# Inner activations as offset float16 integers turned by a DMA, and new instruction orders, in a one-core vision-transformer block

## What is computed

```python
h = patches(x) @ W.T + b                                   # 768 -> 256
c = h @ w1.T + b1
w = softmax((c @ ww.T + bw).reshape(..., 16, 31), -1)      # 16 heads, 31 taps along the image axis
a = layer_norm(h + (causal_tap_sum(w, c) @ w2.T + b2), gamma, beta)
h = _layernorm(h + a)
q1 = act_quant(h)                                          # per row: round(x * 127 / max|x|)
u = silu(q1 @ weight_quant(w_gate).T) * (q1 @ weight_quant(w_up).T)    # 256 -> 1024
out = _layernorm(h + act_quant(u) @ weight_quant(w_down).T)            # 1024 -> 256
```

## Time and profile before

| | us |
|---|---|
| median of 3 runs | 127.66 (127.19 to 128.3) |
| the profiled execution | 127.84 |
| its span, first to last instruction | 125.4 |
| busy in the span: TensorE, VectorE, GpSimd, ScalarE | 112.0, 92.7, 71.3, 65.2 |
| mean granted TensorE clock, share of full speed | 0.989 |

### The profile page before, as it was taken

One profiled execution on the slowest core, in us unless ns is written; L12 is line 12 of the kernel. 1 busy time (PEld: TensorE's weight loads), 2 busy tenths in 40 slices (PEclk: granted clock), 3 DMA queues, 4 the chain that ended last, 5 costly groups with the idle time before them and its releaser, 6 DMA issues.

```text
span 125.4 us, 2349 instructions
## 1 busy us (share of the span) xinstructions
PE 112.0 (89%) x722; PEld 72.2 (58%) x722; DVE 92.7 (74%) x240; ACT 65.2 (52%) x110; POOL 71.3 (57%) x123
## 2 busy tenths in 40 slices
PE   6999989999899999999999999999999984897600
PEld 2377456688358568555855677476676652663400
DVE  5029764387438929999998998996999989699740
ACT  0402139865030834856775469568554775686300
POOL 7990000209002488722886247498978488998870
PEclk9999999999999999999999999999999999999995
DMA  4999999932231011313330220222320001101112
GB/s 91 394 322 408 423 418 423 404 89 19 56 31 10 0 48 14 29 47 33 61 35 6 52 26 3 55 25 57 33 51 5 0 0 42 42 0 42 47 43 82
DMA packets 22313, 12.44 MB, mean 99 GB/s; under 512 B 18013, under 2 KB 20317, under 8 KB 21918
## 3 DMA queue, kind: packets, MB, share of 16 engines
q1 hardware_dynamic: 21504, 10.72, 29.8%
q10 hardware_dynamic: 798, 1.58, 3.9%
HBM read 9.95 MB, written 2.34 MB: 98 GB/s over the span
## 4 chain that ended last, share of the span: by engine, by line
POOL 23%; DVE 13%; PE 12%; issue 8%; ACT 2%; POOLq 1%; DVEq 0%; ACTq 0%
POOL gu L1031 6%; POOL rstd L969 6%; PE bank L400 3%; PE bank L383 3%; POOL f L1038 2%; POOL veps L968 2%; POOL res L1009 2%; PE bank L322 2%; DVE a L734 2%; POOL h L1018 2%; DVE sc L788 1%; POOL shift_out L1007 1%; DVE gu L782 1%; POOL h1b L1026 1%; DVE stats L740 1%
## 5 line engine op out<-in xcount | busy, mean ns | idle before, releaser
L322 PE MATMUL bank<-xT,tokW 128*128 128x256 f32 x96 | 22.8, 387 | 0.3 <-DMA tokW<-in_tokW 0.2
L322 PEld LDWEIGHTS bank<-xT,tokW 128*128 128x128 f32 x96 | 18.3, 194 | 4.7 <-DMA tokW<-in_tokW 1.6
L997 POOL TENSOR_TENSOR taps<-probs,inv_total 128x256 f32<-128x256 f32 x8 | 6.8, 854 | 21.0 <-DVE inv_total L709 21.0
L968 POOL TENSOR_SCALAR veps<-mv 128x1 f32<-128x1 f32 x24 | 5.0, 210 | 22.1 <-DVE mv L719 14.5
L400 PE MATMUL bank<-conv_w,vpad 128*32 128x128 f32 x256 | 15.7, 397 | 0.4 <-DMA conv_w<-shear 0.4
L969 POOL TENSOR_TENSOR rstd<-veps,minus_half 128x1 f32<-128x1 f32 x24 | 14.4, 599 | 2.0
L383 PE MATMUL bank<-wl,h1T 128*128 128x496 f32 x32 | 14.6, 579 | 0.0
L630 ACT ACTIVATE q2T<-bank,minus_magic 128x512 bf16<-128x512 f32 x15 | 10.3, 688 | 5.8 <-PE bank L493 5.7
L493 PE MATMUL bank<-ident,gu 128*128 128x128 f32 x64 | 9.6, 275 | 3.6 <-POOL gu L1031 2.2
L617 ACT ACTIVATE silu<-bank,sc 128x512 f32<-128x512 f32 x16 | 11.0, 687 | 2.7 <-PE bank L453 2.7
L400 PEld LDWEIGHTS bank<-conv_w,vpad 128*32 128x32 f32 x256 | 8.5, 122 | 6.6 <-DMA conv_w<-shear 1.7
(11 more groups left out here) (110 smaller groups left out, 231.1 us busy)
## 6 DMA issues: line engine op xcount, KB each, us to landing
xT<-in_xT SPq DMA_DIRECT2D x3, 768.0 KB, 16.1
w_raw<-in_wg SPq DMA_DIRECT2D x1, 1024.0 KB, 12.6
w_raw<-in_wu SPq DMA_DIRECT2D x1, 1024.0 KB, 14.6
w_raw<-in_wd SPq DMA_DIRECT2D x1, 1024.0 KB, 16.5
shear<-taps SPq DMA_DIRECT2D x8, 128.0 KB, 1.9
conv_w<-shear SPq DMA_DIRECT2D x64, 16.0 KB, 1.9
out_dram<-res SPq DMA_DIRECT2D x8, 128.0 KB
xT<-in_xT ACTq DMA_DIRECT2D x2, 384.0 KB, 5.5
```

The lines of the kernel that those rows point to most:

```text
L322: last = nc.tensor.matmul(ps_embed(pair, m), tokW[:, k, m * P:(m + 1) * P], xT[:, pair, k, :], start=(k == 0), stop=(k == KC_PATCH - 1))
```

## The change

Quantised values are now float16 integers plus 1536 (`STEP`), exact in that type, and all quantised weights and turned activations are float16. For tiles 0 to 5 GpSimd writes q2 (float16) and SP turns the whole 128x1024 tile by one transposing DMA from SBUF to SBUF, straight into q2T; the offset stays in it, and `down` opens with a product of one row, -1536 times the column sums of the down weights, which `down_sums` makes once. Tiles 6 and 7 still go over TensorE, in float16. `centre` moves to ScalarE with its sign turned, the gate and down weights are rounded, clipped and finished on GpSimd, the scale arithmetic is written shorter with a small instruction more on GpSimd (`inner_limit` and the end of `inv_std_mid`), silu is written into `gu`, the first embedding runs by chunks of the inner dimension, and all lists are written anew. The diff, cut to its core:

```diff
-LATE = 5
-WARM_UP = 10
+TP = 6
+WARM_UP = 6
+STEP = 1536.0
 @block.sync
-            sp.dma_start(tokW[:, 0:3, :], tokW_d[:, 0:3, :]).then_inc(tokW_in[0], 16)
-            sp.dma_start(tokW[:, 3:6, :], tokW_d[:, 3:6, :]).then_inc(tokW_in[1], 16)
-            sp.dma_start(w1o[:], w1o_d).then_inc(w1o_in, 16)
+            for k in range(KC_PATCH):
+                sp.dma_start(tokW[:, k, :], tokW_d[:, k, :]).then_inc(tokW_in[k], 16)
+            def turn(t):
+                sp.wait_ge(q2_ok, 2 * t + 2)
+                if t >= 2:
+                    sp.wait_ge(down_ps, t - 1)
+                sp.dma_start(q2T[:, t % 2], q2[:, t % 2, :], transpose=True).then_inc(turned[t % 2], 16)
...
-            put_taps(4); spread(4); put_taps(5); spread(5); put_taps(6); spread(6); put_taps(7); spread(7)
-            store(0); store(1); store(2); store(3); store(4); store(5); store(6); store(7)
+            put_taps(4); spread(4); put_taps(5); spread(5); turn(0); put_taps(6); spread(6); turn(1)
+            put_taps(7); spread(7); turn(2); store(0); turn(3); turn(4); store(1); store(2); turn(5); store(3)
+            store(4); store(5); store(6); store(7)
 @block.tensor
+            def first_embeds():
+                for k in range(KC_PATCH):
+                    pe.wait_ge(tokW_in[k], 16)
+                    pe.wait_ge(x0_in[k], 16)
+                    for m in range(KC):
+                        last = nc.tensor.matmul(ps_embed(0, m), tokW[:, k, m * P:(m + 1) * P], xT[:, 0, k, :],
+                                                start=(k == 0), stop=(k == KC_PATCH - 1))
...
+            def down_sums():
...
+                for k in range(KC_INNER):
+                    last = nc.tensor.matmul(ps_sum, ones16[:], w_q[:, 2, k * D:(k + 1) * D], start=(k == 0),
+                                            stop=(k == KC_INNER - 1))
...
-                nc.tensor.matmul(ps_v, ones_bf[:], bias_mm[:, LOGITS:LOGITS + D], start=True, stop=False)
+                nc.tensor.matmul(ps_v, bias_pick[0:65], bias_mm[0:65, LOGITS:LOGITS + D], start=True, stop=False)
...
+                    if t < TP:
+                        pe.wait_ge(turned[t % 2], 16 * (t // 2 + 1))
+                        pe.wait_ge(sum_read, 1)
+                        nc.tensor.matmul(ps_down, minus_row[0:1], w_sum[0:1], start=True, stop=False)
...
-            project_out(1); embed(3, 0); in_transposes(0); values(2); gate(0, 0); up(0, 0); values(3)
...
+            project_out(1); logits(5); conv(2); residual(2); values(3); in_transposes(0); project_out(2)
+            gate(0, 0); up(0, 0); embed(3, 0); in_transposes(1); residual(3); up(0, 1); gate(0, 1); conv(3)
...
+            project_out(7); up(5, 1); gate(5, 1); down(3, 0); down(3, 1); in_transposes(6); gate(6, 0); up(6, 0)
+            up(6, 1); gate(6, 1); down(4, 0); down(4, 1); in_transposes(7); gate(7, 0); up(7, 0); up(7, 1)
+            gate(7, 1); inner_transposes(6, 0); inner_transposes(6, 1); down(5, 0); down(5, 1); down(6, 0)
+            down(6, 1); inner_transposes(7, 0); inner_transposes(7, 1); down(7, 0); down(7, 1)
 @block.scalar
+            def centre(t):
...
+                nc.scalar.activation(centred[:, t % 2, :], a2[:, t % 2, :], ACT.Identity, bias=mv[:, 1, t % 2, 0:1],
+                                     scale=-1.0).then_inc(centred_ok, 1)
+            for k in range(KC_PATCH):
+                act.dma_start(xT[:, 0, k], xT_d[0, :, k]).then_inc(x0_in[k], 16)
 @block.vector
-            def weight_round(j):
...
             def mid_scales(t):
...
+                at["limit", t] = mark(nc.vector.tensor_scalar(s[:, 1:2], s[:, 0:1], -1.0 / 127.0, s[:, 11:12],
+                                                              ALU.mult, ALU.min))
+                after(at["limit", t])
+                nc.vector.reciprocal(s[:, 7:8], s[:, 1:2]).then_inc(q1_scale_ok, 1)
 @block.gpsimd
             def inv_std_mid(t):
...
+                link(nc.gpsimd.tensor_tensor(rstd[:, 1, t % 2, :], veps[:, 1, t % 2, :].broadcast_to([P, 2]), halves[:],
+                                             ALU.pow))
...
+                nc.gpsimd.tensor_scalar(sc[:, t % 4, 11:12], rstd[:, 1, t % 2, 1:2], -CLIP_EPS / 127.0, 1.0,
+                                        ALU.mult, ALU.mult).then_inc(rstd_mid, 1)
+            def inner_limit(t):
...
+                nc.gpsimd.tensor_scalar(sc[:, t % 4, 10:11], sc[:, t % 4, 7:8], rstd[:, 1, t % 2, 1:2], inner_min[:, 0:1],
+                                        ALU.mult, ALU.mult).then_inc(inner_min_ok, 1)
             def quant_inner(t, half):
-                nc.gpsimd.tensor_scalar(gu[:, t % 2, half, :], gu[:, t % 2, half, :], sc[:, t % 4, 8:9], MAGIC,
-                                        ALU.mult, ALU.add).then_inc(q2_ok, 1)
+                nc.gpsimd.tensor_scalar(q2[:, t % 2, half * HALF:(half + 1) * HALF], gu[:, t % 2, half, :],
+                                        sc[:, t % 4, 8:9], STEP, ALU.mult, ALU.add).then_inc(q2_ok, 1)
...
+            normalise(0); weight_round(0); normalise(1); weight_clip(0); normalise(2); normalise(3)
+            inv_std_attn(0); add_beta(0); weight_round(2); add_beta(1); inv_std_mid(0); weight_clip(2)
+            inv_std_attn(1); weight_finish(0, wq_gate_ok); inv_std_mid(1); add_beta(2); inner_limit(0)
...
```

More of the change, by code:

```diff
@@ L82, in vit_tower @@
         magic = sb("magic", [P, 1])
+        minus_step = sb("minus_step", [P, 1])
+        step = sb("step", [P, 1])
+        halves = sb("halves", [P, 2])
         abs_sum = sb("abs_sum", [P, 3])
@@ new lines, in inner_scales, with down_scale @@
+                at["step", t] = mark(nc.vector.tensor_scalar(s[:, 6:7], s[:, 5:6], 1.0 / 127.0, s[:, 10:11],
+                                                             ALU.mult, ALU.max))
+                after(at["step", t])
+                nc.vector.reciprocal(s[:, 8:9], s[:, 6:7]).then_inc(q2_scale_ok, 1)
+            def down_scale(t):
+                s = sc[:, t % 4, :]
+                after(at["step", t])
+                dve.wait_ge(scale_ok, t + 1)
+                nc.vector.tensor_tensor(s[:, 9:10], s[:, 6:7], s[:, 3:4], ALU.mult).then_inc(down_scale_ok, 1)
@@ new lines, in _ @@
+            inner_scales(2); down_scale(2); mid_absmax(4); attn_stats(5); mid_scales(4); out_scales(4)
+            attn_variance(5); inner(3, 0); attn_centre(5); out_stats(0); out_variance(0); attn_norm(5)
+            inner(3, 1); mid_stats(5); mid_variance(5); inner_absmax(3); mid_absmax(5); inner_scales(3)
+            down_scale(3); attn_stats(6); mid_scales(5); out_scales(5); attn_variance(6); out_stats(1)
+            out_variance(1); attn_centre(6); inner(4, 0); attn_norm(6); inner(4, 1); mid_stats(6)
@@ new lines, in _ @@
+            link(nc.gpsimd.memset(bias_mask[:], -1.0))
+            link(nc.gpsimd.memset(bias_mask[0:32, :], 0.0))
+            link(nc.gpsimd.memset(bias_mask[32:64, 1:2], 0.0))
+            for j in range(3):
+                link(nc.gpsimd.memset(bias_pick[32 * j:32 * j + 1, :], 1.0))
+            link(nc.gpsimd.memset(ident[:], 0.0))
+            link(nc.gpsimd.affine_select(out=ident[:], in_=ident[:], compare_op=ALU.not_equal, fill=1.0, base=0,
+                                         pattern=[[-1, P]], channel_multiplier=1))
```

442 lines of the change are left out of this document (227 added, 215 removed).

## The result

The changed kernel takes 130.75 us (128.88 to 131.56, 4 runs), the kernel before 127.53 beside it (127.19 to 128.30, 4 runs). The ratio is 1.014, interval 1.009 to 1.019: slower, where 122.3 us had been predicted. The profiled execution took 130.16 us, its span 128.2.

The account below looks back on a forecast made before the run. TensorE was taken as the bound up to 101 us, then GpSimd and VectorE. Start -1.7, transposes -4.7, longer chain +1.4 and tail -0.3 sum to -5.3, giving 122.3 us from the median of 127.66; range 118.5 to 126.3.

Parts of the forecast that it names:

- All these are queues that TensorE outlasts up to 101 us: Step on the other engines: TensorE bounds until 101 us, so VectorE's relief counts nothing and GpSimd's +10 us fits.
- +1.4 together: Tile 7's uncovered chain at 98 to 109 us, one hop longer, with GpSimd fuller; bounds -2.2 and +4.
- -5.3: Predicted total change in us over the whole kernel, the sum of -1.7, -4.7, +1.4 and -0.3.
- Rival (a): GpSimd becomes the bound: 69 us of work from 39.6 us on, at 87% busy, gives 124.7; chance 0.22.
- The transposes, -4.7: TensorE's work up to the end of gate(7, 1) falls by 4.7 us net; bounds -3.9 and -4.9.
- I count it whole: Step that credits all 4.7 us saved on transposes to the total, since TensorE hardly waits in that stretch.
- The start, -1.7: Chunked first loads and six warm-ups end the embeddings at 9.4; ww at 10.0 leaves 1.7 gain; bounds 0.5 and 2.3.
- The turn, 3 us,: Transposing DMA of one tile from SBUF to SBUF takes 3 us, between 1.9 and 9.2; cost 0, up to +2.
- rival (c): Slow turning DMAs for tiles 0 to 5 make down wait: 132 us at 12 us each; chance 0.10.
- Rival (d): No change: TensorE waits as long as it saves, chiefly for gate weights from GpSimd; 126.5 to 127.5, chance 0.10.
- Rival (b): TensorE's gap in 101.6 to 111.5 us closes since VectorE has 11 us less: 118.8 us; chance 0.12.
- The tail, -0.3: Last tile: shorter scales and transposes, against GpSimd taking the last rstd later; bounds -1.2 and +1.

Follow-up runs that it names:

- run 1: Changed kernel with the w1o transfer issued on SP's queue ahead of ww instead of on ScalarE's behind the patch chunks; 131.39 us, ratio 1.029.
- run 3: Changed kernel with the six turning DMAs undone: all eight tiles transposed on TensorE in float16 and copied by ScalarE; 130.48 us, ratio 1.024.
- run 4: Changed kernel with only GpSimd's order altered: inv_std_attn(7) ahead of scale_h3(5), inv_std_mid(7) ahead of result(2) and add_h3(3); 128.23 us, ratio 1.003.
- run 5: Changed kernel with 14 useless products put ahead of the last tile's transposes, where TensorE waited 3.83 us; 128.84 us, ratio 1.011.
- run 7: Changed kernel with the earlier start: transfers in halves, w1o ahead of ww on SP, ten warm-ups, new product order kept; 127.81 us, ratio 1.002.
- run 2: Changed kernel without inner_limit and the end of inv_std_mid on GpSimd, constant lower bounds, so part is not computed; 124.97 us, ratio 0.979.
- run 6: Changed kernel with the scale work back on VectorE, one power on GpSimd, no inner_limit, everything computed; 124.36 us, ratio 0.975.
- run 9: Changed kernel with the scale work back on VectorE and the turning DMAs undone (edits of run 6 and run 3); 128.34 us, ratio 1.003.
- run 10: Changed kernel with the scale work back on VectorE and the first transfers as before (edits of run 6 and run 7); 124.89 us, ratio 0.978.
- run 12: Kernel of run 11 with 8 useless products in TensorE's list ahead of the last tile's transposes; 123.70 us, ratio 0.969.
- run 11: Changed kernel with the edits of run 6, run 7 and run 4, a third result buffer, tile 6's residual sum on VectorE; 123.81 us, ratio 0.970.

## Why the prediction was wrong, step by step

**The failed step** is "All these are queues that TensorE outlasts up to 101 us" together with the term that followed from it, "+1.4 together, bounds -2.2 ... and +4" for the longer chain and the fuller GpSimd. Of the 8.5 us between -5.3 and +3.2 the start makes 2.7 (below), and the other 5.8 belong here and to the transposes that it swallowed. What the runs show in its place: from `quant_inner(2, 1)` on, at some 79 us, GpSimd hardly waits any more, and the length of its list from there sets the end. From the start of that instruction to the end of the last power, in us of the profiled executions:

| kernel | from, to | length | waits for others | without them |
|---|---|---|---|---|
| changed | 79.06, 124.67 | 45.6 | 1.4 | 44.2 |
| run 1, w1o first | 81.87, 126.26 | 44.4 | 0.2 | 44.2 |
| run 3, turning undone | 78.88, 126.16 | 47.3 | 3.1 | 44.2 |
| run 4, order | 78.48, 122.61 | 44.1 | 0.2 | 43.9 |
| run 5, hole filled | 78.28, 122.66 | 44.4 | 0.2 | 44.2 |
| run 7, start as before | 77.63, 122.60 | 45.0 | 1.0 | 44.0 |
| run 2, work left out | 78.27, 119.46 | 41.2 | 1.1 | 40.1 |
| run 6, scales on VectorE | 77.49, 118.50 | 41.0 | 1.3 | 39.7 |
| run 9, turning undone too | 78.47, 122.78 | 44.3 | 4.5 | 39.8 |
| run 10, runs 6 and 7 | 77.68, 119.91 | 42.2 | 2.7 | 39.5 |

Whatever is done to TensorE, its clock or the order, the last column stays at 44; only work taken off GpSimd changes it. What relieving GpSimd gives back is 6.4 us by run 6, of which 1.6 are an earlier start in the profiled execution, or 2.9 over a start that is firm in both (run 10 against run 7). The load was forecast well (81 us, measured 82.1), but it was set against TensorE's only as a sum over the whole kernel. The three small steps of tiles 6 and 7 behind large ones are how TensorE and VectorE come to wait; that their order alone costs the time is not shown.

**Rival (a)** had the mechanism, and 0.22, but was priced at 124.7, by spreading GpSimd's work over everything from 39.6 us on at 87%. Its rows give 34.55 of 41, that is 84%, and with that the same sum makes 127.3. Of the 7.4 us that GpSimd got behind 39.6 (66.05 for 58.61), 5.3 were done before 81 us, but it also stood still there for 12.0 of 41.4 us, mostly because its list waited for results of other engines. So the full stretch began near 79 us and not at 39.6, and from 81 us on 36.7 us of work (17.72 + 8.63 + 8.76 + 1.56) took 47.2; the rest is 1.4 of waits, 3.5 behind its last power, and the short gaps between instructions.

**The transposes, -4.7.** The size was near. In the changed kernel two q1 transposes take 0.11 us of TensorE's queue, as predicted, but a product of one row holds it for 0.21 (92.49 to 92.70) and not for 0.11; with that the sum is -4.2. "I count it whole" was wrong in this kernel: in run 3, where 48 float16 transposes are back on TensorE, the time is between 0.3 less and 1.0 more, and in run 9 against run 6 it is 4.0 more. (Neither puts the f32 transposes back, so they don't measure the -4.7 itself.) TensorE was ahead until 91 us, and its lead was then waited away in one hole of 3.83 us. It had been said that nothing covers tile 7's chain at 98 to 109; with TensorE's work ahead of it shorter, the hole was bound to be longer by what TensorE saved, unless that chain came earlier too. That is what the sum lacked.

**The start, -1.7.** It came out as +1.0. Both ends of the range (0.5 and 2.3 of gain) assumed that chunks cost no rate and that ww, not w1o, would be the last to land. Undoing it gives 2.9 by run 7 (1.4 in the profiled executions), nothing on top of run 6 by run 10.

**The turn, 3 us,** landed in 3.1, and rival (c) is out. Its place on SP did no harm but for 1.4 us of waits, and none in run 6. **Rival (d)** is out: no wait for weights ahead of the first gate product. **Rival (b)**, 118.8: the gap in 101.6 to 111.5 grew instead.

**The tail, -0.3:** the power of the last tile, 1.5 us late before, was 3.45 late, 1.20 of it for a store; in runs 4, 5 and 7, which have no such wait, the last result waits 2.38, 2.59 and 1.78. The bound of +1 was too small for the same reason as the main term.

**Not in the sum at all:** the clock. It fell behind the hole, and the last tile's products ran at the lower level. Filling the hole gives nothing in run 12, and what it gives in run 5 the trace puts down to the start and a store: GpSimd ends last whatever TensorE does.

**Open:** how much of the scatter of the changed kernel's runs is the start's (only profiled executions show it); what the turning gains in the changed kernel; and why run 10 stays 0.5 above run 6 (124.89 and 124.36). There the clock may count: it was at 0.57 and 0.79 from 104 to 112 us, and GpSimd waited 1.8 and 0.4 us for ScalarE's `scaled_down`. It was not tried apart.

**The version to keep** is run 11, 123.81 us: the change with its scale work on VectorE, loads in halves, three result buffers. Run 12's filler adds nothing that can be measured.

**A slip of reading:** where the prediction says what bounds the kernel, it writes that TensorE "idles 33.14 of 34.00" and so on; these are its busy times. The 1.66 us of idle time that it takes from them are right.

## What to carry to other kernels

When work moves from a full engine to one with room, don't ask only whether the totals fit. Find the instruction behind which the fuller engine no longer waits for anybody, and add up its list from there to the end: here 44 us from 79 us on, on an engine that was busy 64% of the span. If that comes out later than the path you are shortening, it is the bound, and every us that goes onto it there is paid in full. What another engine saves is then lost in its next wait. Compare the starts of the profiled executions before a difference is given to an edit: here the start moved by up to 1.6 us from one to the next. And undo a part again after the bottleneck is gone: undoing the turning DMA cost 1.0 us at most in one kernel, by the times, and 4.0 us in the other.
